# Cross attention on one core: the negated score maxima are split and turned on VectorE instead of on TensorE

## What is computed

```python
qn, kvn = layer_norm(x), layer_norm(ctx_1024)              # each with gamma and beta
Q, K, V = qn @ Wq, kvn @ Wk, kvn @ Wv                      # 16 heads of 32
attn = softmax(Q @ K.T / sqrt(32))                         # per head, 512 x 512
out  = x + gelu((attn @ V) @ Wo + bo)
```

## Time and profile before

| what | value |
|---|---|
| median of 3 runs | 3279.45 us (3277.87 to 3283.18) |
| profiled execution, its span | 3277.9 us |
| granted TensorE clock, mean | 0.998 |
| PE busy | 3244.4 us, 99% |
| DVE, ACT, POOL busy | 2256.6, 2276.0, 2315.9 us (69%, 69%, 71%) |
| one batch, one step | about 102 us, about 25.6 us |

### The profile page before, as it was taken

The page is one execution under the profiler, slowest core; times in us unless marked ns, Lnnn a source line. Parts: engine busy times, 40 slices in busy tenths (PEclk is TensorE's granted clock), DMA queues, the critical chain, the costliest instruction groups (busy, mean ns, idle before and its releaser), DMA issues.

```text
span 3277.9 us, 60424 instructions
## 1 busy us (share of the span) xinstructions
PE 3244.4 (99%) x16611; PEld 2140.0 (65%) x16611; DVE 2256.6 (69%) x4769; ACT 2276.0 (69%) x3985; POOL 2315.9 (71%) x1544
## 2 busy tenths in 40 slices
PE   8999999999999999999999999999999999999998
PEld 5566666666666666666666666666666666666664
DVE  6667667676676676666766766766667667667664
ACT  5677666777767777667767667776777676677765
POOL 3676776777677767777776677777767776777665
PEclk9999999999999999999999999999999999999999
DMA  6655656566556556565665566565656655666653
GB/s 142 89 106 106 107 103 113 90 108 106 105 102 103 108 106 105 103 116 87 110 107 103 105 100 109 107 102 103 119 83 111 106 106 106 98 109 106 103 78 76
DMA packets 186492, 340.15 MB, mean 104 GB/s; under 512 B 20561, under 2 KB 20577, under 8 KB 186466
## 3 DMA queue, kind: packets, MB, share of 16 engines
q1 hardware_dynamic: 186000, 339.03, 60.2%
q10 hardware_dynamic: 466, 0.80, 0.2%
HBM read 104.87 MB, written 33.55 MB: 42 GB/s over the span
## 4 chain that ended last, share of the span: by engine, by line
PE 97%; DVE 1%; ACT 1%; issue 1%; DMA 0%; POOL 0%; SPq 0%; ACTq 0%; POOLq 0%; DVEq 0%
PE gen L856 43%; PE score L883 15%; PE score L876 15%; PE ctx L903 14%; PE gen L847 4%; PE gen L943 4%; PE gen L965 1%; DVE maxes L706 0%; DMA k_stack<-k_nat 0%; ACT q_stack L617 0%; PE score L788 0%; DVE stats L725 0%; ACT probs L563 0%; PE gen L837 0%; POOL probs L475 0%
## 5 line engine op out<-in xcount | busy, mean ns | idle before, releaser
L475 POOL TENSOR_TENSOR probs<-probs 128x1024 f32<-128x1024 f32 x762 | 1802.0, 2396 | 291.9 <-PE ctx L903 285.7
L706 DVE TENSOR_REDUCE maxes<-score 128x1 f32<-128x512 f32 x2048 | 1295.8, 682 | 202.8 <-PE score L883 201.9
L563 ACT ACTIVATE probs<-score 128x512 f32<-128x512 f32 x2048 | 1086.3, 621 | 140.5 <-PE score L876 134.4
L883 PE MATMUL score<-k_stack,q_stack 96*128 96x512 f32 x2048 | 762.1, 413 | 3.4 <-DVE maxes L706 1.8
L876 PE MATMUL score<-q_stack,k_stack 128*128 128x512 f32 x2048 | 697.8, 407 | 6.3 <-ACT q_stack L617 6.3
L883 PEld LDWEIGHTS score<-k_stack,q_stack 96*128 96x128 f32 x2048 | 378.9, 189 | 217.6 <-ACT probs L563 83.9
L876 PEld LDWEIGHTS score<-q_stack,k_stack 128*128 128x128 f32 x2048 | 374.5, 189 | 200.8 <-DVE maxes L706 59.3
L903 PE MATMUL ctx<-probs,v_sb 128*32 128x512 f32 x4096 | 492.6, 599 | 0.0
L856 PE MATMUL gen<-w_v,cT 128*128 128x512 f32 x1536 | 462.2, 396 | 0.0
L856 PE MATMUL gen<-cT,w_k 128*128 128x512 f32 x1536 | 461.9, 400 | 0.2 <-DVE q_nat L688 0.2
L856 PE MATMUL gen<-xT,w_q 128*128 128x512 f32 x1536 | 448.6, 394 | 3.0 <-issue 0.4
(11 more groups left out here) (89 smaller groups left out, 2765.7 us busy)
## 6 DMA issues: line engine op xcount, KB each, us to landing
k_stack<-k_nat SPq DMA_DIRECT2D x384, 256.0 KB, 7.8
q_stack<-q_nat SPq DMA_DIRECT2D x381, 256.0 KB, 5.6
tok<-in_x SPq DMA_DIRECT2D x132, 256.0 KB, 10.4
tok<-in_ctx SPq DMA_DIRECT2D x128, 256.0 KB, 11.0
res<-in_x SPq DMA_DIRECT2D x124, 256.0 KB, 2.6
out<-res SPq DMA_DIRECT2D x124, 256.0 KB, 2.1
probs<-in_L_xattn_Wq SPq DMA_DIRECT2D x1, 1024.0 KB, 8.1
probs<-in_L_xattn_Wk SPq DMA_DIRECT2D x1, 1024.0 KB, 10.4
```

Source lines behind the costliest of these rows:

```text
L475: pool.tensor_tensor(probs[:, c + 1, heads], probs[:, c + 1, heads], probs[:, c, heads], ALU.add).then_inc(pool_added, 1)
L563: act.activation(probs[:, n, part, :], score_at(s, "st", i)[:], ACT.Exp, scale=SCALE).then_inc(exp_done, 1)
L706: dve.tensor_reduce(maxes[:, u1 % 2, SROW + i:SROW + i + 1], score_at(s, "s", i)[:], AX_X, ALU.max, negate=True).then_inc(max_done, 1)
L883: pe.matmul(score_bank(pe, b, s, "s", i)[:, :], q_stack[0:KROWS, u1 % 2, n, P * part:P * (part + 1)], k_stack[0:KROWS, u1 % 2, n, :], star ...
```

## The change

The transpose on PE, the split on ACT and the merge on DVE (`m`, `mh`, `ml`) are gone. All is done in `md` on DVE, in six instructions: a copy of the 16 maxima to fp32r (high parts), a subtraction (low parts), and four transposes of 32x32 blocks, each from its own 32 partitions into partitions 96 to 127 of `max_hl`. `mx` on ACT now waits for these four. The list `GEN` has 28 entries in place of 32. The masks `cut_sign` and `low_row`, made once at the start, are gone too, and `maxes` is one buffer of 16 columns. Cut to its core:

```diff
 ORDER = {
     "pe": (
-        "... pv m k o*2 k o k*2",
+        "... pv k o*2 k o k*2",
     "act": (
-        "... st*4 mh mx*4 k",
-        "... norm x*2 gelu mh gelu mx*4 split",
+        "... st*4 mx*4 k",
+        "... norm x*2 gelu gelu mx*4 split",
     "dve": (
-        "... s*5 md ml ln*2 k ob",
-        "... s ob s*4 md ob ml",
-        "s ob s*6 zt s zr zb cn s k s*7 md q ml",
-        "k zt zr zb cn q s*16 md ml",
+        "... s*5 md ln*2 k ob",
+        "... s ob s*4 md ob",
+        "s ob s*6 zt s zr zb cn s k s*7 md q",
+        "k zt zr zb cn q s*16 md",
...
-        if _part == 0 and _kind in ("q", "k", "m", "z"):
+        if _part == 0 and _kind in ("q", "k", "z"):
...
                         if kind == "md" and valid(b1):
                             wait(dve, max_done, 16 * (t1 + 1))
-                            dve.tensor_reduce(maxes[:, u1 % 2, SROW + SHIFTS // 2:P],
-                                              maxes[:, u1 % 2, SROW:SROW + SHIFTS // 2].unsqueeze(2), AX_X,
-                                              ALU.max).then_inc(max_copied, 1)
-                        if kind == "ml" and valid(b1):
-                            wait(dve, max_cut_done, t1 + 1)
+                            dve.tensor_copy(max_split[:, 0:SHIFTS // 2], maxes[:]).then_inc(max_high, 1)
+                            wait(dve, max_high, t1 + 1)
+                            dve.tensor_tensor(max_split[:, SHIFTS // 2:SHIFTS], maxes[:], raw(max_split[:, 0:SHIFTS // 2]),
+                                              ALU.subtract).then_inc(max_low, 1)
                             wait(dve, shift_rows, NC * t1)
-                            dve.scalar_tensor_tensor(out=max_hl[SROW:P, :], in0=gen_at("m", u1)[SROW:P, 0:P],
-                                                     scalar=low_row[SROW:P, 0:1], in1=raw(max_cut[SROW:P, :]),
-                                                     op0=ALU.mult, op1=ALU.add).then_inc(free["m"], 1)
+                            wait(dve, max_low, t1 + 1)
+                            for g in range(P // SHIFTS):
+                                rows = slice(SHIFTS * g, SHIFTS * (g + 1))
+                                dve.transpose(max_hl[SROW:P, rows], raw(max_split[rows, :])).then_inc(max_turned, 1)
...
-                        if kind == "m" and valid(b1):
-                            bank = gen_bank(pe, b, "m", u1)
-                            wait(pe, max_copied, t1 + 1)
-                            pe.matmul(bank[:, 0:P],
-                                      maxes[:, u1 % 2, :], ident[:], start=True, stop=True,
-                                      is_transpose=True).then_inc(full["m"], 1)
```

More of the change, by code:

```diff
@@ L53 @@
         "q*3 v q*2 v q v st*2 v*2 s st v s st s v*2 st s st s z v st*3 s v*2 st*2 s st k v s*4 pv st s st*2 o s "
[1 row of a table removed]
[1 row of a table added]
         "o st*2 o st*3 q st q*4 st q st*3 z x k*3 x st*2 x st k*2 s k st s st*2 pv s x s x s x s pv s x s*2 o*3 "
[1 row of a table removed]
[1 row of a table added]
         "o*4 s o s k s k s st k s st z st s st s q st q st s st*2 k st*3 k s st k st*4 pv s*2 q s q s*2 q s*2 q "
[1 row of a table removed]
[1 row of a table added]
         "k q k v q v k*2 st*3 k st*2 q st*2 k q st q st q st*2 z st*4 v st v s*3 pv s*2 v s*2 v s*2 v s v s*2 v*2 "
[1 row of a table removed]
[1 row of a table added]
     ),
     "act": (
[4 rows of a table removed]
+        "q st*4 v st*8 norm v split norm*2 st*4 mx*4 k",
+        "st*6 gelu q st x st*2 norm st*4 x k st*2 norm x norm st x*2 norm x norm x*2 gelu gelu mx*4 split",
+        "gelu st*12 k split st*4 q mx*4",
+        "st*6 k st*5 q st*4 split st v*2 mx*4",
     ),
     "dve": (
[4 rows of a table removed]
[4 rows of a table added]
     ),
@@ L208, in build @@
         ones = sb("ones", [P, P])
[L209 to L213, removed]
+        maxes = sb("maxes", [P, SHIFTS // 2])
+        max_split = sb("max_split", [P, SHIFTS], F32R)
+        max_hl = sb("max_hl", [P, P])
         chunk_mask = sb("chunk_mask", [P, NC])
@@ L232, in build @@
         gen = [ps(f"gen{i}") for i in range(NGEN)]
-        full = {k: sem(f"{k}_in_psum") for k in "vomzxqk"}
-        free = {k: sem(f"{k}_out_of_psum") for k in "vomzxqk"}
+        full = {k: sem(f"{k}_in_psum") for k in "vozxqk"}
+        free = {k: sem(f"{k}_out_of_psum") for k in "vozxqk"}
         st_full = sem("st_full")
@@ L243, in build @@
         x_hi = sem("x_hi")
-        max_cut_done = sem("max_cut_done")
-        max_copied = sem("max_copied")
+        max_high = sem("max_high")
+        max_low = sem("max_low")
+        max_turned = sem("max_turned")
         shift_rows = sem("shift_rows")
@@ L440, in _ @@
             pool.memset(minus_half[:], -0.5).then_inc(consts, 1)
-            pool.memset(low_row[:], 0.0).then_inc(consts, 1)
-            pool.memset(cut_sign[:], 1.0).then_inc(consts, 1)
             pool.memset(act_out[:], 0.0).then_inc(act_out_free, 1)
-            pool.wait_ge(consts, 5)
+            pool.wait_ge(consts, 3)
             pool.affine_select(out=ident[:], in_=ident[:], compare_op=ALU.not_equal, fill=1.0, base=0,
                                pattern=[[-1, P]], channel_multiplier=1).then_inc(consts, 1)
[L447 to L452, removed]
             def prepare(b, s):
@@ L609, in batch @@
                                            bias=bias_k[:, u2:u2 + 1]).then_inc(k_hi, 1)
[L610 to L614, removed]
                         if kind == "mx" and valid(b1):
-                            wait(act, free["m"], NU * b1 + u1 + 1)
+                            wait(act, max_turned, HU * (NU * b1 + u1 + 1))
                             act.activation(q_stack[SROW:P, u1 % 2, :, P * n:P * (n + 1)],
-                                           raw(max_hl[SROW:P, :]).unsqueeze(1).to_broadcast([SHIFTS, HU, P]),
+                                           max_hl[SROW:P, :].unsqueeze(1).to_broadcast([SHIFTS, HU, P]),
                                            ACT.Identity, scale=chunk_mask[SROW:P, n:n + 1]).then_inc(shift_rows, 1)
@@ L625, in _ @@
         def _(dve):
-            dve.memset(maxes[:], 0.0)
             dve.memset(z_inv[:], 1.0).then_inc(stack_used, 2)
-            dve.wait_ge(consts, 8)
+            dve.wait_ge(consts, 4)
             dve.tensor_reduce(chunk_mask[:], ident[:].rearrange("p (g c) -> p c g", c=NC), AX_X,
@@ L702, in batch @@
                             i = NC * n + part
-                            if i == 0:
-                                wait(dve, full["m"], t1 - 1)
                             wait(dve, s_full, 16 * t1 + i + 1)
-                            dve.tensor_reduce(maxes[:, u1 % 2, SROW + i:SROW + i + 1], score_at(s, "s", i)[:], AX_X, ALU.max,
+                            dve.tensor_reduce(maxes[:, i:i + 1], score_at(s, "s", i)[:], AX_X, ALU.max,
                                               negate=True).then_inc(max_done, 1)
@@ L779, in _ @@
         def _(pe):
-            pe.wait_ge(consts, 8)
+            pe.wait_ge(consts, 4)
             pe.wait_ge(cols_loaded, 16 * 4)
@@ L886, in batch @@
                             wait(pe, ctx_split, NU * B - 2)
-                            for kind2, count in (("z", NU * B - 1), ("m", NU * B), ("q", NU * B), ("k", NU * B),
+                            for kind2, count in (("z", NU * B - 1), ("q", NU * B), ("k", NU * B),
                                                  ("x", 2 * NC * B), ("v", NC * B), ("o", NC * (B - 1))):
```

2 lines of the change are left out of this document (1 added, 1 removed), and 16 rows, old and new, of the table ORDER.

## The result

The changed kernel takes 3748.57 us (median of 4 runs, 3743.6 to 3753.82), the kernel before 3281.31 us beside it; the ratio is 1.1424 (1.141 to 1.1438). That is 467 us more, 15 us a batch. The direction was as forecast, and so was the question of who waits for whom; the size was not: 3635 was predicted, and 3748.57 lies above the stretch of 3570 to 3710 given for two waits a block, and above the whole range, which ended at 3720.

What follows compares the result with a forecast made beforehand. The prediction took PE's stream, busy 99%, as the bound. DVE's waits for POOL would stall PE 2.4 + 3.35 + 2.35 + 3.5 = 11.6 us a batch, 360 in 31 batches on 3278: 3638, given as 3635, range 3258 to 3720.

Steps and rivals of the forecast that it cites:

- two waits a block: DVE's copy and subtraction each wait for a POOL instruction at every block of maxima: 3635 us, 3570 to 3710, chance 0.36.
- PE is the bound before, and `m` costs little: PE's stream, busy 99%, sets the time; removing `m` gains only 0.07 us in steps 0 and 2.
- The gain at the loop's turn: On PE in step 3, the loop's branch runs while `pv` runs out: 0.07 to 0.38 us gained, 0.38 taken.
- The first `st` of steps 1 and 3: On PE, an earlier `mx` lets these start sooner: up to 0.2 us gained each.
- The block without waits: DVE's copy, subtraction and four transposes, waiting for nobody: 1.25 us, bounds 0.8 and 1.6, 1.35 taken.
- Who waits: DVE's copy and subtraction each wait for POOL's present instruction; one `add` is 2.36 us; blocks take 3.65 to 5.95 us.
- The stalls: PE's delays from the longer blocks in steps 0 to 3: 2.4, 3.35, 2.35 and 3.5 us a batch.
- The sum: PE's four delays make 11.6 us a batch, times 31 batches 360 us, added to 3278: 3638, given as 3635.
- One wait: Rival: in each block DVE waits only for the rest of one POOL instruction: 3420 to 3480 us, chance 0.24.
- No wait: Rival: DVE always goes before POOL, so gains and delays nearly cancel: 3276 to 3290 us, chance 0.20.
- Faster: Rival: overlapping transposes make DVE's block 0.8 to 0.9 us, DVE going first: 3247 to 3268 us, chance 0.13.
- POOL keeps the path: Rival: POOL holds it through a run of `add`, blocks of 10 us in steps 0, 2, 3: over 4000 us, chance 0.07.

Runs made afterwards that it cites:

- the kernel with small additions: The changed kernel with POOL's six additions a unit cut to one column in 512, DVE's instructions unchanged: 3291.53 us, ratio 1.0031.
- the kernel of reduces: The changed kernel with copy and subtraction both made of reduces: 3456.75 us; with one implied DVE wait also left out, 3292.47 us.
- The kernel with the stalls filled: The changed kernel with useless matmuls added on PE in the stalls of all four steps: 3629.66 us, ratio 1.1061.
- both kernels of 290 records: Copy and subtraction as reduces in the changed kernel, 3456.75 us; the shorter-loop version with bias first, plus eight small DVE writes a batch, 3416.69 us.

## Why the prediction was wrong

- *PE is the bound before, and `m` costs little.* Right. The gain at the loop's turn was taken as 0.38; it is 0.43. The first `st` of steps 1 and 3 gave 0.3 and 0.1 in the kernel with small additions, where 0.2 each were taken.
- *The block without waits.* Right: 1.35 was taken, 1.40 measured. The transposes don't overlap: 0.204 each, four in 0.915. The Trainium skill ("VectorE: DVE Perf Modes", section "Two Vector instructions with no wait between them") says that an instruction whose output or input starts in another 32 partitions than the last one's is held until all before it are done. The trace agrees: each transpose starts some 0.03 us after the last one has ended, while in the kernel of reduces the second reduce, on the same partitions as the first, starts 0.08 before the first has ended.
- *Who waits.* Right in both parts: DVE waits for POOL, and a second time between copy and subtraction. No row of before showed either. The blocks were forecast as 4.3, 3.65, 3.85 and 5.95 us in steps 0 to 3 and are 4.0, 3.6, 3.6 and 5.6. The three with a fresh `add` before the subtraction were 0.3 too long, since the wait for a fresh `add` ends 2.32 after the subtraction's start and its own 0.17 lies in that.
- *The stalls.* 2.4, 3.35, 2.35 and 3.5 us were forecast; by the lag they are 2.1, 3.8, 2.3 and 4.0. The kernel with the stalls filled puts their sum at 348 us, net of the gains; 360 was forecast. The last of the four, 4.0, includes the 0.43 that the loop's turn has just gained, so PE is 3.5 later there than before, as forecast. That the sum came so close is in part luck: step 1's block cost 0.45 more than forecast, step 0's 0.3 less.
- *The sum.* This is the step that failed. "11.6 x 31 = 360, and 3278 + 360" charges PE's stalls and runs everything else at the old speed. All the prices of matmuls in it are those of a clock of 0.998, in a kernel in which PE never rested. A forecast of four rests of 2 to 4 us a batch had to ask what PE does behind them. It runs at half its clock for 330 us in all, and that cost 119 us. Neither the sum, nor a rival, nor the range had a term for it; with it, 3635 + 119 = 3754, beside 3749 measured. The 119 was measured afterwards and could not have been read from a row of before, where 17 us ran at the lower clock; but the term had to be named and the range widened for it.
- *The rivals.* "One wait" was priced at 3420 to 3480. The two kernels that have one came out at 3449 (the kernel before with a copy) and 3541 (the changed kernel with the copy as a reduce), both with stretches at the lower clock (102 and 218 us) that the price had left out too. "No wait" was low by 2 us at its upper end (3276 to 3290 against 3291.5 and 3292.5). "Faster" fell: the transposes don't overlap. "POOL keeps the path" is wrong as a rule, but the one copy of 4.70 us is a case of it.

## What to carry to other kernels

On DVE, a copy between SBUF tiles and an operation with two SBUF operands wait for POOL's present instruction (here up to 2.4 us for 0.17 of work), and two such with a wait between them for two. Where POOL is busy with long instructions, take a reduce (0.16 to 0.19 every time here) or an operand in PSUM (the low part of q, 0.75 with POOL at work and 0.74 without), however small the tile. When a forecast gives PE rests that it did not have, price the lower clock behind them too: here 119 us on top of stalls of 348. And count a looping engine's instructions before adding to them.

## What was not expected of the hardware

- **A loop that just doesn't fit.** With 282 records in a turn of DVE's loop, its instructions were fetched once (13 or 14 packets). With 290 there were 159 packets, so they seem to have come anew at each turn, and DVE stood still for some 8 us at each: 143 to 164 us in all. The Trainium skill ("Runtime: NRT & Kernel Launch", section "Instruction fetch mechanics") says that a branch whose target is outside the loaded window forces a fetch before work goes on; the packets and the 8 us agree. Whether the length decides or where the loop lies is open: both kernels of 290 records had more in front of the loop, too. PE's loop has 633 to 667 records and shows none of it.
- **The clock behind short rests.** With four rests of 2 to 4 us a batch, 330 us ran at the lower level, against 17 before. With the rests filled the granted clock was 0.996.
- **The loop's branch hides.** Behind `m` it cost PE 0.3 us a turn. In the changed kernel it stands behind a `pv`, whose last matmul starts 0.52 us before whatever follows it, and the first product comes 1.85 us behind the start of `pv` there as at every other place: the branch costs nothing that shows.
